# A fused recurrence, expert layer, attention and feed-forward kernel: shorter attention preparation, another feed-forward order, and a new schedule of the last routing

## What is computed

```python
x = x + recurrence(layernorm(x), cond, ctx)   # per sequence: softmax attention over ctx inside a tanh RNN, 64 steps
x = x + experts(layernorm(x))                 # sigmoid router, 4 of 8 groups, 8 of 64 experts; plus a shared expert
x = x + block(layernorm(x), cond, ctx)        # self-attention, cross-attention, GELU-gated feed-forward
x = x + (layernorm(x) @ W.T + pooled @ disha)

def adaln(x, t, w, b):                        # ahead of each of the block's three parts
    scale, shift = split(t @ w + b)
    return layernorm(x) * (1 + scale) + shift
```

## Time and profile before

| | |
|---|---|
| median of 3 runs | 1079.64 us |
| profiled execution | 1078.22 us |
| its span, first to last instruction | 1076.5 us |
| PE, DVE, ACT, POOL busy | 943.2, 732.7, 478.1, 564.5 us |
| mean granted TensorE clock | 0.89 of full |

### The profile page before, as it was taken

How to read it: one execution, slowest core, us unless ns; L and a number is a source line. 1 busy time by engine, 2 the same in 40 slices (tenths; PEclk the granted TensorE clock), 3 DMA queues, 4 the chain that set the end, 5 groups by cost and what they waited for, 6 DMA issues and landing times. The chain is left out here.

```text
span 1076.5 us, 29797 instructions
## 1 busy us (share of the span) xinstructions
PE 943.2 (88%) x12378; PEld 631.0 (59%) x12378; DVE 732.7 (68%) x1789; ACT 478.1 (44%) x889; POOL 564.5 (52%) x519
## 2 busy tenths in 40 slices
PE   3598987699999999999989968889999899998786
PEld 3377776455555555555434426677777667776554
DVE  5635455557676767767866656778787777777664
ACT  2232223132323233233222216677777677775652
POOL 3688801033434343434545555666766666667763
PEclk9555555589999999999999988999999999998998
DMA  9120024232222222322344410000000000000001
GB/s 251 34 74 1 2 50 86 57 84 76 63 80 65 79 60 80 82 62 79 98 103 118 118 39 2 2 2 3 3 3 3 2 3 3 3 3 2 2 2 40
DMA packets 46205, 51.68 MB, mean 48 GB/s; under 512 B 22102, under 2 KB 36727, under 8 KB 46071
## 3 DMA queue, kind: packets, MB, share of 16 engines
q1 hardware_dynamic: 43152, 48.78, 17.6%
q10 hardware_dynamic: 2918, 1.01, 0.5%
HBM read 48.20 MB, written 1.57 MB: 46 GB/s over the span
## 5 line engine op out<-in xcount | busy, mean ns | idle before, releaser
L712 POOL TENSOR_TENSOR ex<-ex,xn 128x512 f32<-128x512 f32 x128 | 162.4, 1269 | 224.2 <-ACT thcb L960 109.3
L960 ACT ACTIVATE thcb<-ps 128x512 f32<-128x512 f32 x132 | 78.9, 598 | 207.0 <-PE ps L1787 206.0
L793 POOL TENSOR_TENSOR wu<-encC,wu 128x1024 f16<-128x1024 f32 x64 | 137.4, 2161 | 57.8 <-ACT encC L1028 57.8
L1794 PE MATMUL ps<-ex,wd 128*128 128x512 f32 x256 | 138.8, 625 | 0.5 <-DVE xT L1385 0.5
L1373 DVE SCALAR_TENSOR_TENSOR ex<-thcb,ps 128x512 f32<-128x512 f32 x132 | 90.6, 686 | 59.6 <-ACT thcb L960 55.6
L1787 PE MATMUL ps<-xnT,wg 128*128 128x512 f16 x384 | 105.3, 383 | 2.1 <-DVE ex L1379 2.0
L1732 PEld LDWEIGHTS ps<-eb,encC 128*128 128x128 f16 x3072 | 86.8, 99 | 32.1 <-DVE eb L1242 19.5
L1787 PE MATMUL ps<-xnT,wu 128*128 128x512 f16 x384 | 104.1, 380 | 0.0
L1021 ACT CAST wu<-ps 128x1024 f16<-128x1024 f32 x64 | 64.9, 1015 | 85.1 <-PE ps L1878 85.1
L787 POOL TENSOR_TENSOR wd<-wd,a_sum 128x512 f32<-128x512 f32 x64 | 66.5, 1042 | 67.2 <-DVE a_sum L1494 67.2
L1843 PE MATMUL ps<-wg,M 128*128 128x128 f16 x1536 | 97.3, 221 | 2.1 <-DVE wg L1463 2.1
(11 more groups left out here) (309 smaller groups left out, 1792.7 us busy)
## 6 DMA issues: line engine op xcount, KB each, us to landing
xn<-coef_rows SPq DMA_DIRECT2D x128, 256.0 KB, 3.9
thcb<-in_L_ffn_Wg SPq DMA_DIRECT2D x8, 256.0 KB, 3.2
thcb<-in_L_ffn_Wu SPq DMA_DIRECT2D x8, 256.0 KB, 3.3
wd<-in_L_ffn_Wd SPq DMA_DIRECT2D x2, 1024.0 KB, 10.2
xtok<-in_x SPq DMA_DIRECT2D x4, 256.0 KB, 6.1
thcb<-in_ctx SPq DMA_DIRECT2D x2, 512.0 KB, 11.3
wu<-in_L_xcond_attn_wq SPq DMA_DIRECT2D x2, 512.0 KB, 11.0
wu<-in_L_xcond_attn_wk SPq DMA_DIRECT2D x2, 512.0 KB, 10.6
```

Source lines behind the costliest of these rows:

```text
L712: nc.gpsimd.tensor_tensor(hid[:, side(m, n), :], gu[:, side(m, n), :], other, ALU.mult)\
L793: nc.gpsimd.tensor_tensor(z[:, 1, 8 * u:8 * u + 8, :], a_Zc[:, u], z[:, 0, 8 * u:8 * u + 8, :], ALU.subtract)\
L960: nc.scalar.activation(th[:, side(m, n), :], bank(side(m, n)), ACT.Tanh, scale=0.5 / WSCALE)\
L1794: mm(bank(5), wd[:, n, :] if n < PAIRS else swd[:, :], hid[:, side(m, n), :], start=(n == 0), stop=(n == UNITS - 1)).then_inc(s["y_ready"], 1)
```

## The change

The diff touches five places. (1) `LAST`, a table of its own for the last routed part, spreads the routing over gaps 0 to 33 in smaller pieces; and behind the recurrence POOL's product of a unit waits until the next unit's tanh is ready. (2) The last `add_units` comes in two pieces, the first 8 sequences ahead; ACT, POOL and the first transposes go on after the first. Statistics and normalisation of stage 0 read the transposed rows in PSUM bank 6, and ACT copies them to SBUF behind the normalisation. (3) `prep_rstd` for a = 0 computes 1 / sqrt(var + eps (var + eps)) at once, and the root for xin after the release. `prep_norm` and `gather` stand ahead of `sums(n, 1)` where j = 1; scale and shift follow each other there, with the scaled values in place in PSUM. (4) The same for the feed-forward's norms (`f_modulate`). The x3 sums get buffers that are free earlier and move from items 28 to 30 and unit 6 into items 15, 23 and 28 and unit 7. (5) `f_rstd1(1)` stands ahead of the last item's normalisations on POOL and `f_norm1(1)` ahead of the first gelu on ACT; transposes, last product and output of a finished block come one unit later.

```diff
--- before
+++ after
@@ -218,6 +218,8 @@
...
 
+        STAGES = ((0, 0), (1, 0), (0, 1), (2, 0), (1, 1), (3, 0), (2, 1), (3, 1))
+        ITEMS = 4 * len(STAGES)
         few = sfc[:, :, :].rearrange("p n e -> p (n e)")
...
@@ -240,7 +242,7 @@
...
         f_hs = [xT_f[:, (2 + i) * CT:(3 + i) * CT].bitcast(F16).rearrange("p (x n) -> p x n", x=2) for i in range(2)]
-        f_x3 = [tiles(ctxT[:, k * CT:(k + 1) * CT]) for k in range(CH)]
+        f_x3 = [tiles(v) for v in (Hc[:, :, :].rearrange("p t b -> p (t b)"), blocks[:, :], ctxT[:, 0:CT], ctxT[:, CT:2 * CT])]
         f_split = [(w1[:, i * CT:(i + 1) * CT], [w1h[:, x, i * CT:(i + 1) * CT] for x in range(2)]) for i in range(2)]
...
@@ -258,6 +260,7 @@
...
 
+        X3_AT = {4 * STAGES.index((0, 1)) + 7: 0, 4 * STAGES.index((1, 1)) + 7: 1, ITEMS - 4: 2}
         F_NT = {FC * (k - 1) + 1 if k > 1 else 2: k for k in range(1, CH)}
...
@@ -282,8 +285,6 @@
...
         QUADS = NPAIR // 4
-        STAGES = ((0, 0), (1, 0), (0, 1), (2, 0), (1, 1), (3, 0), (2, 1), (3, 1))
-        ITEMS = 4 * len(STAGES)
         a_Gs = [t.bitcast(F16).rearrange("p (x b h q) -> p x b h q", x=2, b=2, q=64)
...
@@ -497,6 +498,11 @@
...
             PARTS += [(m, 0, TPC // 2, GAPS * m + GAPS // 2, HALF), (m, TPC // 2, TPC, GAPS * (m + 1), HALF)]
+        LAST = {0: ("project",), 2: ("residual",), 3: ("stats",), 6: ("x1T",), 8: ("xn2T",), 10: ("router",), 12: ("sig0",),
+                13: ("sig1",), 14: ("sfc",), 15: ("halves",), 17: ("quarters",), 18: ("pairs",), 19: ("top2",), 21: ("more",),
+                22: ("equal",), 23: ("rank",), 25: ("under",), 26: ("mask",), 27: ("pick",), 28: ("take0", "take1"),
+                30: ("sum",), 31: ("inverse",), 32: ("coef",), 33: ("coefT",)}
+        PARTS[-1] = PARTS[-1][:4] + (LAST,)
         PRO = {}
...
@@ -740,6 +746,8 @@
...
                         pool.wait_ge(s["en_ready"], t + 2)
+                    elif t >= T and (m, n) != chunk_units[-1]:
+                        pool.wait_ge(s["th_ready"], m * UNITS + n + 2)
                     unit(m, n)
...
@@ -761,15 +769,14 @@
...
                     return
+                a_settle(nc.gpsimd.tensor_tensor(r1, r0, eps, mul))
+                a_settle(nc.gpsimd.tensor_tensor(r1, r1, var, add))
+                nc.gpsimd.tensor_tensor(r2, r1, rsqrt, pow_).then_inc(s["a_rstd"], 1)
                 a_settle(nc.gpsimd.tensor_tensor(r0, r0, rsqrt, pow_))
-                a_settle(nc.gpsimd.tensor_tensor(r1, r0, r0, mul))
-                a_settle(nc.gpsimd.tensor_tensor(r1, r1, var, mul))
-                a_settle(nc.gpsimd.tensor_tensor(r1, r1, eps, add))
-                a_settle(nc.gpsimd.tensor_tensor(r1, r1, rsqrt, pow_))
-                nc.gpsimd.tensor_tensor(r2, r1, r0, mul).then_inc(s["a_rstd"], 1)
 
...
                 g, a = STAGES[k]
+                pool.wait_ge(s["a_x2"], g + 1)
                 xin, x2 = (t[:, 4 * g:4 * g + 4, :] for t in (a2tok, x2tok))
...
@@ -842,6 +849,8 @@
...
                     f_rstd1(0)
+                if n == ITEMS - 1:
+                    f_rstd1(1)
                 if ahead and j == 1:
...
@@ -850,10 +859,8 @@
...
                     f_hi_lo(0)
-                if n == ITEMS - 1:
-                    f_rstd1(1)
-                if n >= ITEMS - 4 and n < ITEMS - 1:
-                    f_x3_sum(n - (ITEMS - 4))
+                if n in X3_AT:
+                    f_x3_sum(X3_AT[n])
 
...
@@ -865,7 +872,7 @@
...
                     f_rstd1(k + 2)
-                if u == FC + 2:
+                if u == FC + 3:
                     f_x3_sum(CH - 1)
...
@@ -986,6 +993,8 @@
...
                 act.wait_ge(s["a_x2T"], g + 1)
+                if k == 0:
+                    act.wait_ge(s["a_nrm"], 1)
                 nc.scalar.copy(x2tok[:, 4 * g:4 * g + 4, :], bank(6 if k < 2 else 7).rearrange("p (j d) -> p j d", d=P))\
...
@@ -1104,9 +1113,10 @@
...
 
+            f_norm1(1)
             for u in range(FF + FF_LAG):
                 k, c = divmod(u, FC)
-                if c == 1 and k >= 2:
+                if c == 2 and k >= 2:
                     f_n2T_in(k - 2)
...
@@ -1115,12 +1125,11 @@
...
                     f_hid_hi(u)
-                if u == 0:
-                    f_norm1(1)
                 if u in F_NT:
...
                     f_norm1(k + 2)
+            f_n2T_in(CH - 2)
             f_n2T_in(CH - 1)
@@ -1382,8 +1391,10 @@
...
                 dve.wait_ge(s["x1T_ready"], parts_done(m))
-                V.tensor_tensor(dst, dst, bank(5).rearrange("p (t b) -> p t b", b=B), add)\
-                 .then_inc(s["x2_ready"], 1)
+                y = bank(5).rearrange("p (t b) -> p t b", b=B)
+                for b in (range(0, B),) if m < CH - 1 else (range(0, 8), range(8, B)):
+                    b = slice(b[0], b[-1] + 1)
+                    V.tensor_tensor(dst[:, :, b], dst[:, :, b], y[:, :, b], add).then_inc(s["x2_ready"], 1)
 
...
@@ -1417,14 +1428,22 @@
...
 
+            def prep_rows(k, j):
+                g, a = STAGES[k]
+                if k == 0:
+                    return bank(6)[:, j * P:(j + 1) * P]
+                return (a2tok if a else x2tok)[:, 4 * g + j, :]
+
             def prep_stats(k):
...
                     dve.wait_ge(s["a_res"], 1 + STAGES.index((g, 0)))
+                elif k == 0:
+                    dve.wait_ge(s["a_x2T"], 1)
                 else:
...
                 for j in range(4):
-                    a_mark(V.bn_stats(a_st[:, j, :], (a2tok if a else x2tok)[:, 4 * g + j, :]))
+                    a_mark(V.bn_stats(a_st[:, j, :], prep_rows(k, j)))
                 if k and STAGES[k - 1][1] == 0:
...
@@ -1436,27 +1455,23 @@
...
             def prep_norm(k):
-                g, a = STAGES[k]
                 dve.wait_ge(s["a_rstd"], k + 1)
...
                 for j in range(4):
-                    last = V.tensor_scalar(a_nrm[:, j, :], (a2tok if a else x2tok)[:, 4 * g + j, :], a_mv[:, j, 0:1],
-                                           a_rs[:, 2, j:j + 1], sub, mul)
+                    last = V.tensor_scalar(a_nrm[:, j, :], prep_rows(k, j), a_mv[:, j, 0:1], a_rs[:, 2, j:j + 1], sub, mul)
                     if j < 3:
...
 
-            def prep_h32(k, part):
+            def prep_h32(k):
                 g, a = STAGES[k]
                 scale, shift = (ss[:, 2 * a + i, 8 * g:8 * g + 8].unsqueeze(2).broadcast_to([P, 8, 64]) for i in range(2))
-                h8 = a_h32.rearrange("p (b t) -> p b t", t=64)
+                n8, h8 = (v.rearrange("p (b t) -> p b t", t=64) for v in (bank(7), a_h32))
                 dve.wait_ge(s["a_nT"], k + 1)
-                if part == 0:
-                    V.tensor_tensor(h8, bank(7).rearrange("p (b t) -> p b t", t=64), scale, mul).then_inc(s["a_hm"], 1)
-                else:
-                    dve.wait_ge(s["a_hm"], k + 1)
-                    V.tensor_tensor(h8, h8, shift, add).then_inc(s["a_h32"], 1)
+                V.tensor_tensor(n8, n8, scale, mul).then_inc(s["a_hm"], 1)
+                dve.wait_ge(s["a_hm"], k + 1)
+                V.tensor_tensor(h8, n8, shift, add).then_inc(s["a_h32"], 1)
 
...
@@ -1525,19 +1540,15 @@
...
 
-            def f_scale(k):
-                scale = ss[:, 4, 8 * k:8 * k + 8].unsqueeze(2).broadcast_to([P, 8, T])
+            def f_modulate(k):
+                scale, shift = (ss[:, i, 8 * k:8 * k + 8].unsqueeze(2).broadcast_to([P, 8, T]) for i in (4, 5))
                 n8, h8 = (v.rearrange("p (b t) -> p b t", t=T) for v in (bank(nT_bank(k)), f_h32))
                 dve.wait_ge(s["f_nT"], k + 1)
+                V.tensor_tensor(n8, n8, scale, mul).then_inc(s["f_hm"], 1)
                 if k:
                     dve.wait_ge(s["f_h_lo"], k)
-                V.tensor_tensor(h8, n8, scale, mul).then_inc(s["f_hm"], 1)
-
-            def f_shift(k):
-                shift = ss[:, 5, 8 * k:8 * k + 8].unsqueeze(2).broadcast_to([P, 8, T])
-                h8 = f_h32.rearrange("p (b t) -> p b t", t=T)
                 dve.wait_ge(s["f_hm"], k + 1)
-                V.tensor_tensor(h8, h8, shift, add).then_inc(s["f_h32"], 1)
+                V.tensor_tensor(h8, n8, shift, add).then_inc(s["f_h32"], 1)
 
...
@@ -1582,8 +1593,7 @@
...
             prep_norm(0)
-            prep_h32(0, 0)
-            prep_h32(0, 1)
+            prep_h32(0)
             prep_h_low(0)
...
@@ -1593,12 +1603,8 @@
...
                     f_stats1(0)
-                if n == ITEMS - 2:
-                    f_shift(0)
                 if ahead and j == 1:
                     prep_stats(k + 1)
-                if ahead and j == 2:
-                    prep_h32(k + 1, 1)
                 if n >= 1:
...
@@ -1611,22 +1617,24 @@
...
                     G_low(n + 1, 3)
-                if 0 <= n < ITEMS:
-                    sums(n, 1)
+                if n >= 1 and j == 1:
+                    gather(n - 1)
                 if ahead and j == 1:
...
                     f_first_norm()
-                if n >= 1:
+                if 0 <= n < ITEMS:
```

(25 more changed lines are left out.)

## The result

The changed kernel takes **1042.18 us** (median of 4, 1041.81 to 1043.25) against 1079.56 for the kernel before (median of 4, 1078.63 to 1080.21): a ratio of 0.9656, 95% interval 0.9639 to 0.9673. The forecast was 1043.6. Its profiled execution took 1041.81 us.

What follows compares the result with a forecast made beforehand. It took TensorE (PE) to bound most of the time, leaving PE's waits and the slow clock behind them to save. 6.0 + 4.4 + 16.2 + 5.9 + 3.5 = 36.0 off 1078.22, plus 1.42: 1043.6 us, range 1036 to 1059.

Steps and rivals of the forecast that it cites:

- (1) tail: Tail beside the last routing: held GpSimd products no longer stretch VectorE's routing operations; 6.0 us saved, bounds 2.5 and 7.0.
- (2) start: Start of attention: split add, statistics from PSUM, shorter root chain, uncovered normalisation; 4.4 us saved, bounds 3.4 and 4.7.
- (3) items j = 1 and two successors: Attention items preparing the next stage: PE starts earlier, five items save 7.0 and two pairs 9.2; 16.2 us, bounds 9 and 18.
- (4) item 29 and next: Item preparing the feed-forward: x3 sums move away, 4.6 us saved, and 1.3 in the next item; 5.9, bounds 2.8 and 6.5.
- (5) feed-forward: Feed-forward: first normalisation moved saves 0.6, later transposes 2.4, a second wait 0.4; 3.5 us in all, bounds 0 and 7.
- the signs named: Trace marks listed for a right forecast, among them no routing operation at L1343 or L1362 over 0.5 us.
- 4.4 us after a DVE add: Start of attention: sign that PE's first L1827 comes some 4.4 us after a DVE add shorter than before.
- becomes a wait for gelu(0): Feed-forward start: PE's wait of 3.12 for f_norm1(1) turns into one for the first gelu; 0.6 us saved.
- costs nothing, as the two take the same place: Feed-forward start: f_rstd1(1) goes ahead of GpSimd's last products, into the place the x3 sum leaves; no cost.
- A: Rival: PE's waits only move, to GpSimd's products behind the postponed sums; half the items' gain goes, 1054.6 us, chance 0.13.
- B: Rival: VectorE falls behind in the tail and routing is stretched as before; tail saves 2.5, 1047.1 us, chance 0.11.
- C: Rival: the held product is late for `down` in all 53 tail units; 37 us lost, 1086.6 us, chance 0.03.

Runs made afterwards that it cites:

- no_hold: The changed kernel without GpSimd's new wait in the tail, new routing table kept; one traced run, tail 2.94 us longer, span 1043.3 us.
- old_table: The changed kernel with the old routing table for the last part, GpSimd's new wait kept; one traced run, tail 5.12 us longer, span 1048.2 us.
- late_shift: The changed kernel with attention's scaling (PSUM to SBUF) and shift apart again, the shift one item later; one traced run, span 1043.6 us.
- item_order: The changed kernel with VectorE's old order in the j = 1 items (sums, normalisation, gather); median 1055.37 us, ratio 0.9785 to the kernel before.
- x3_late: The changed kernel with the four x3 sums in their old places, new buffers kept; median 1047.81 us, ratio 0.9710 to the kernel before.
- early_gather: The changed kernel with gather(31) ahead of the fourth hidden unit's low half on VectorE; one traced run, feed-forward stage 1.09 us shorter, span 1044.6 us.

## Why the prediction was right, and where only its sum was

Against the profiled execution the terms came out so (before less after, from the landmarks of the trace):

| term | forecast | measured | by the experiments |
|---|---|---|---|
| (1) tail | 6.0 | 5.74 | of 5.86 by stage: table alone 2.92, hold alone 0.74, 2.2 only together |
| (2) start | 4.4 | 4.28 | shorter chain 1.65; scaling in PSUM 0.93 of what it would else lose |
| (3) items j = 1 and two successors | 16.2 | 16.69 | order 9.67; the other 7.0 not separated, and 3.3 of each pair not in every item with the same code |
| (4) item 29 and next | 5.9 | 6.06 | order 2.57; x3 sums 0.65 lost with the new order, PE's wait 1.39 shorter with the old one |
| (5) feed-forward | 3.5 | 3.49 | x3 sums 3.2 (4.3 with a fall of the clock); first normalisation −2.05; transposes 0 |

The closeness of single terms is in part luck. The changed kernel's profiled execution has the shortest start (18.05) of the eleven traces with that code, which reach 18.92, and the shortest FF of seven, which reach 54.13. With the longest, (2) would have come to 3.4 and (5) to 1.9.

**(1)** The mechanism (an operation that starts with the product ends with it) and the size were right. The prediction gave the gain to the hold and called the table a spreading of work that fits anyway; no_hold and old_table show that the hold is worth little without the table, and that the table gives half. Worked out right was the place of the overfill, sum and inverse; it costs 1.1 us. One of the signs named was missed by it: L1371, which was L1362, takes 1.12 and not under 0.5.

**(2)** To PE's first transposes 4.41 were gained, which is the forecast's 4.4 (the sign "4.4 us after a DVE add" was not: they come 4.92 behind the end of the add's second piece). Statistics from PSUM took 0.89 for four (0.1 allowed), the chain's 1.6 was measured as 1.65, and the normalisation took 1.36 where 1.2 stood. The shift was costed at nothing and would have taken 1.54, but for the scaling in PSUM. The first groups of G run at half clock for a part, as they did before.

**(3)** Five items were to gain 1.4 each and gained 1.46 to 1.48; the two pairs were to gain 4.6 each and gained 4.61 and 4.74. The cause named for the pairs was in part wrong: late_shift shows that the shift's place is worth nothing by itself. With the old order but the short chain the pair takes 22.2, with the new order and the long chain 21.5 to 21.6, and with both old things 25.66. But items 9 and 10 of the kernel before have both old things as well, and took 12.74 and 9.63 at full clock. PE's wait was 1.96 in item 9, 2.13 in item 1 and 1.95 in item 17; behind the last two the clock fell. The rows of items 9 and 17:

```profile
765.76 0.66 PE L1827 MATMUL ps<-ident,wd 128*128 128x128 f32 x4 [1.96 <-DVE wd L1501]
...
853.03 0.69 PE L1827 MATMUL ps<-ident,wd 128*128 128x128 f32 x4 [1.95 <-DVE wd L1501]
```

In item 10 the shift started 0.17 us ahead of GpSimd's product and took 0.68; in item 18, after the fall, it started 0.17 behind it and took 2.50. So 3.3 of each pair's gain is a fall of the clock and what follows it, which the same code had in two places and not in a third. The prediction took both for granted; the changed kernel's waits there are 0.5 to 0.7, and no trace with them has a fall. Long chain and old order together, with the shift early, wasn't run, and only one execution of the kernel before was traced.

**(4)** The sum of 5.9 and its two parts are right: PE comes to the transposes 2.32 earlier (2.3 was said), and the other 2.32 of the item are clock. The x3 sum was a cause, but not one that was needed: in the old order it adds 1.38 to the normalisation (3.88 against 2.50 in item_order), in the new order it costs nothing (x3_late), while the order alone gives 2.57. The prediction named the x3 sum and not the order. The 1.4 of item 30 were put down to the shift; it took 2.16 beside a product before and stands in item 29 now, but it wasn't tried alone.

**(5)** Here the number is right by errors that cancel, and by the clock. Its parts as written add up to 3.4, not 3.5. The first normalisation's move was put at +0.6, and costs 2.05: the step by which PE's wait of 3.12 "becomes a wait for gelu(0)" counted PE's waits and not ACT's queue, in which 2.43 of idling now stand ahead of 1.28 of table load. The middle was put at +2.4 for the postponed transposes; they give nothing, and the short norm, a consequence of the x3 sum's place, gives it (1.0 in x3_late; in the kernel before 3.0 are lost at that place, with a fall of the clock in it). The x3 sums' part at the start, 2.2, was missed: the prediction had said that the root "costs nothing, as the two take the same place". The end was to be unchanged and came out 0.91 shorter: 0.45 in PE's transposes and 0.21 in its last product are clock (0.66 against 1.11, 1.87 against 2.08), which the other runs show to vary by as much.

Of the rivals, A (waits only move) is seen in the feed-forward: PE's wait for the gather of item 31 went from 0.72 to 2.95, one of 1.10 stands at 1011.18, and in early_gather one of 1.12 takes the place of the 2.95. B is what old_table and no_hold look like, at 2.9 to 5.1 us. C left no trace: at L1801 PE waited 0.9 us for L718 in the whole execution.

## What to carry to other kernels

When an operation of one engine holds up another's, a rule of when the one may start and a plan that puts no more on the other than a gap holds may pay only together (here 0.74, 2.92 and 5.86 us); test them in the four combinations. When a queue's order is changed, add up the waits of every engine in that stage, not those of the bound one: the engine that sets the pace two units on may be another. Cut traces into stages at landmarks before comparing kernels: here it made 0.1 us readable in tail and items under a clock that moves whole executions by 4.7. And before a slow place is explained, look for the same code elsewhere in the trace: item 9 stood beside items 1 and 17.

## What the runs showed of the hardware

- The first rise of TensorE's clock came at 221.9 us or up to some 12 us later, with the same work, and moved the landmark behind it by up to 4.7 us.
- The first groups of G took 4.32 to 5.30 us in different runs of changed kernels, by when the clock returned from 1.2 to 2.4 GHz.
- In the feed-forward the clock fell behind some waits of PE in one execution and not in another of the same code (52.5 against 54.1 us).
- In one execution of the kernel before the clock fell behind a wait of PE of 1.95 us (item 17) and not behind one of 1.96 in the same code (item 9).
- A DVE operation that reads and writes the same PSUM bank in place took 0.70 us for 128x512; one from PSUM to SBUF took 0.69.
- The same shift with both inputs in SBUF took 1.54 beside a GpSimd product, and 0.69 with one input in PSUM.
- A `tensor_scalar` over two columns was held like operations with two SBUF inputs: 1.12 us instead of 0.17.
